# The first image's stages placed four rounds earlier in a hand-made software pipeline

## What is computed

```python
x = x + conv_attention(group_norm(x))   # 1x1 qkv, 5x5 depthwise + grouped 1x1, linear attention, 1x1, batch norm
x = x + conv3x3(group_norm(x), sign(weight))
t = to_tokens(x)                        # 256 tokens x 64
t = t + attention(layer_norm(t))        # 16 heads, three branches: causal, 128 selected tokens, window 32
t = t + moe(layer_norm(t))              # 8 experts, top 2 per token
t = t + linear_attention(layer_norm(t)) # 8 heads of 16
t = t + moe(layer_norm(t))              # 8 experts, routing by image; needs the mean over tokens, and
                                        # the expert loads over all eight images
```

## Time and profile before

| | us |
|---|---|
| median of three runs | 1038.12 |
| lowest and highest | 1030.46, 1038.23 |
| the profiled execution | 1033.71 |
| its span | 1031.8 |
| PE busy | 895.3 (87%) |
| DVE busy | 598.2 (58%) |
| ACT busy | 436.4 (42%) |
| POOL busy | 205.0 (20%) |
| mean granted TensorE clock | 0.97 |

### The profile page before, as it was taken

The page is one execution under the profiler, slowest core; times in us unless marked ns, Lnnn a source line. Parts: engine busy times, 40 slices in busy tenths (PEclk is TensorE's granted clock), DMA queues, the critical chain, the costliest instruction groups (busy, mean ns, idle before and its releaser), DMA issues.

```text
span 1031.8 us, 22157 instructions
## 1 busy us (share of the span) xinstructions
PE 895.3 (87%) x9150; PEld 613.3 (59%) x9150; DVE 598.2 (58%) x1687; ACT 436.4 (42%) x734; POOL 205.0 (20%) x274
## 2 busy tenths in 40 slices
PE   5878789899989899989988999899899989877877
PEld 4766565566656666666656666566565655644553
DVE  6353545663597358745875477637773655462456
ACT  0002235443454245425543464445445535524654
POOL 1011100120123012311241124102411231140122
PEclk9999899999999999999999999999999989997988
DMA  7000000000000000000100000100000000021000
GB/s 190 2 6 1 1 7 21 22 22 26 22 22 23 26 22 22 23 27 6 30 30 26 1 22 27 37 2 22 22 26 23 26 32 23 21 69 30 2 1 22
DMA packets 27140, 25.31 MB, mean 25 GB/s; under 512 B 16480, under 2 KB 22240, under 8 KB 26912
## 3 DMA queue, kind: packets, MB, share of 16 engines
q1 hardware_dynamic: 27040, 23.90, 8.1%
HBM read 19.16 MB, written 4.72 MB: 23 GB/s over the span
## 4 chain that ended last, share of the span: by engine, by line
PE 63%; DVE 18%; ACT 9%; issue 5%; DMA 2%; POOL 2%; SPq 0%; DVEq 0%; POOLq 0%; ACTq 0%
PE ring L904 9%; PE side_a L624 5%; PE pv L943 5%; PE pv L925 4%; ACT pr L1160 4%; PE ring L859 4%; PE heads L847 3%; DVE rden L1639 3%; PE side_a L631 2%; PE heads L884 2%; PE ring L899 2%; PE ring L867 2%; DVE img L1357 2%; PE heads L844 2%; PE side_a L668 2%
## 5 line engine op out<-in xcount | busy, mean ns | idle before, releaser
L1160 ACT ACTIVATE pr<-ring 128x1024 f32<-128x1024 f32 (+1 forms) x128 | 120.9, 944 | 118.5 <-PE ring L908 64.9
L904 PE MATMUL ring<-kq 64*128 64x256 f32 (+2 forms) x1280 | 137.7, 342 | 0.8 <-ACT kq L1205 0.5
L904 PEld LDWEIGHTS ring<-kq 64*128 64x128 f32 x1280 | 93.0, 188 | 44.9 <-issue 35.8
L1197 ACT ACTIVATE kq<-ring 128x896 f32<-128x896 f32 x64 | 58.8, 919 | 92.7 <-PE ring L859 92.7
L1624 DVE TENSOR_REDUCE toks<-heads 128x2 f32<-128x512 f32 x64 | 44.2, 691 | 86.4 <-PE heads L889 85.2
L1649 DVE SCALAR_TENSOR_TENSOR ob<-pv,all_gates,scale 128x256 f32<-128x256 f32 x96 | 46.3, 482 | 77.5 <-issue 33.3
L1639 DVE RECIPROCAL rden<-pv 128x256 f32<-128x256 f32 x32 | 56.1, 1753 | 40.6 <-PE pv L925 40.6
L1629 DVE TENSOR_REDUCE toks<-heads 128x4 f32<-128x512 f32 x64 | 44.2, 690 | 53.4 <-PE heads L884 53.0
L1205 ACT ACTIVATE kq<-ring 128x256 f32<-128x256 f32 x64 | 24.4, 382 | 115.8 <-PE ring L867 115.8
L559 POOL TENSOR_TENSOR toks<-ta,tb 128x128 f32<-128x128 f32 (+1 forms) x96 | 40.3, 439 | 160.2 <-DVE tb L1614 160.2
L859 PE MATMUL ring<-early,toks 128*128 128x128 f32 x448 | 62.2, 279 | 11.2 <-ACT pr L1160 10.5
(11 more groups left out here) (379 smaller groups left out, 1763.5 us busy)
## 6 DMA issues: line engine op xcount, KB each, us to landing
scale<-branch_scale SPq DMA_DIRECT2D x128, 96.0 KB, 2.3
branch_scale<-rden SPq DMA_DIRECT2D x32, 128.0 KB, 1.7
late<-in_late SPq DMA_DIRECT2D x1, 2158.5 KB, 8.3
xin<-in_x SPq DMA_DIRECT2D x16, 64.0 KB, 2.2
pr<-in_prep SPq DMA_DIRECT2D x1, 602.0 KB, 3.8
y<-ob SPq DMA_DIRECT2D x8, 64.0 KB, 1.9
kq<-in_masks SPq DMA_DIRECT2D x1, 480.0 KB, 8.4
toks<-in_final SPq DMA_DIRECT2D x1, 434.0 KB, 4.8
```

The lines of the kernel that those rows point to most:

```text
L904: m = pe.matmul(ring[:, j, at:at + nq], kq[rows, k, key0:key0 + P], kq[rows, k, Q + q_:Q + q_ + nq], start=r % 2 == 0, stop=at > P)
L1160: act.activation(out, in_, ACT.Exp, scale=SCALE).then_inc(S("exp_done"), 1)
L1197: act.activation(kq[:, k, :], flat[:, 0:WIDE], ACT.Copy).then_inc(S("turned"), 1)
```

## The change

The first image's front starts at round -4 instead of 0. Its heads start 16 and its back 48 rounds later than its front, as before, so at 12 and 44 instead of 16 and 48. The other images keep their rounds, and the loop runs from -4.

```diff
-        FRONT_AT = [ROUNDS * n for n in range(B)]
-        HEADS_AT = [ROUNDS * n + ROUNDS for n in range(B)]
-        REST_AT = [ROUNDS * n + 3 * ROUNDS for n in range(B)]
-        TIMES = range(REST_AT[-1] + ROUNDS)
+        LEAD = 4
+        FRONT_AT = [ROUNDS * n - (0 if n else LEAD) for n in range(B)]
+        HEADS_AT = [at + ROUNDS for at in FRONT_AT]
+        REST_AT = [at + 3 * ROUNDS for at in FRONT_AT]
+        TIMES = range(-LEAD, REST_AT[-1] + ROUNDS)
```

## The result

| | before | after |
|---|---|---|
| median, us | 1034.29 (4 runs, 1029.95 to 1038.23) | 1060.97 (4 runs, 1054.40 to 1069.24) |
| ratio after to before, 95% interval | | 1.0263 [1.0167, 1.036] |
| the profiled execution, its span | 1033.71, 1031.8 | 1064.22, 1062.3 |
| PE, DVE, ACT, POOL busy | 895.3, 598.2, 436.4, 205.0 | 915.7, 599.8, 436.1, 204.8 |
| mean granted TensorE clock | 0.970 | 0.947 |

What follows compares the result with a forecast made beforehand. PE was taken as the bound, except in rounds 16 to 31, bound by the second image's serial front chain. Terms +10.3 - 5.8 - 2.4 = +2.1 us gave 1035.8, placed at 1038 towards the runs' median; range 1028 to 1049.

Steps and rivals of the forecast that it cites:

- the worst bound of the sum: Low clock costs again (+4.5), scale loads 3 us more, the back's start 3 us more: +12.6 us.
- the sum of +2.1: Total over rounds 16 to 63: 10.3 - 5.8 - 2.4 = +2.1 us against the profiled execution.
- The path to round 16, parallel from round 64 on, only the three stretches matter: Time up to 70.17 us unchanged, same order from round 64; the whole effect lies between 70 and 335 us.
- Rounds 16 to 31, +10.3: First stretch: 13.2 us of the first image's head work moves in; 63.9 us grows to 74.2.
- At full clock 12.9 + 4.9: Rounds 24 to 27: existing work at full clock plus four fills, and 1.8 of waits, makes 19.6 us.
- The ropes ahead of statistics and image writes: Rounds 16 to 19: DVE's rope products precede the second image's statistics and image writes; its conv starts 4.8 us later.
- Rounds 32 to 47, -5.8: Second stretch: 13.2 us of head work leaves, 3.8 us of denominators and weighings enters; net -5.8 us.
- The new wait for the scale load: Rounds 36 to 39: the second weighing has too little other PE work ahead of it; 2 us of new wait.
- Rounds 48 to 63, -2.4: Third stretch: PE work falls 3.8 us, 1.4 lost as the first image's back precedes the fourth image's mean; -2.4 us.
- The front's chain takes the work for nothing: Rival: idle time in rounds 16 to 31 absorbs the moved work; 1027 to 1032 us; chance 0.12.
- The clock: Rival: clock falls to half again in rounds 24 to 27; +4.5, total +6.6, 1042 us; chance 0.18.
- The collision at round 48: Rival: rounds 48 to 51, a late scale load stalls the fourth image's front; over +10 us; chance 0.12, including several waits.

Runs made afterwards that it cites:

- e1: The change, but the first image's back stays at round 48, so only its front and heads start four rounds earlier; ratio to before 1.0143, mean span 1045.6 us.
- e2: The change, but POOL takes the first image's 5.4 us power two rounds later; ratio to before 1.0195, mean span 1051.4 us.
- f1: The change, but DVE does the second image's statistics and image writes ahead of the ropes in rounds 16 and 17; ratio to before 1.0244, mean span 1056.6 us.
- f2: The change without the filler matmuls of the second image's front; ratio to before 1.0183, mean span 1050.3 us.
- g1: The change with back left at round 48, DVE's statistics and writes ahead of ropes in rounds 16 and 17, no second-image fillers; ratio to before 1.0057.
- f3: The kernel before without the filler matmuls of the second image's front; ratio to before 1.0045, mean span 1036.1 us.

## Why the prediction was wrong

Against the four runs the forecast of 1038 missed by 23, and its range ended 12 us short. The measured change lies beyond the worst bound of the sum too (+12.6). Worked from the profiled executions, the sum of +2.1 stands against +31.4 us at round 64. Two steps failed above all. The low clock of before was taken as gone after the change, 5.3 us that came off the first stretch, and it grew instead. And POOL was not followed to its new place, where its power makes PE wait 5.28 us.

**Step by step.**
- *The path to round 16, parallel from round 64 on, only the three stretches matter.* Right.
- *Rounds 16 to 31, +10.3.* Measured +23.4 in the profiled execution. This is the first step that failed, and its place in the text is "At full clock 12.9 + 4.9": it took the low clock of before (0.89 in this stretch, 5.3 us by the prediction's own figures) as gone after the change. It stayed and grew: 0.82. The sizes at full clock were near, a little low. With 0.38 us for each microsecond at low clock (from e1 and after), the four blocks of after come to 22.8, 11.9, 19.2 and 21.6 us, where the text has 23.4, 12.4, 19.6 and 18.8; the last is off, by 2.8 us. With before's 63.9 brought to full clock in the same way (58.6) the order costs 16.9 us; the text has 15.6, "so 13.2 us of work makes it 15.6 longer". By 0.23, the price in time, it costs 19.5. e1, whose clock of 0.90 is nearly that of before, shows it almost without a correction: 82.64 us and 0.9 from 70.17 to its start, against 63.91, is +19.6. So beside the 5.3 us of clock some 4 us of waits are missing.
- *The ropes ahead of statistics and image writes.* Right in kind, 4.1 us over whole runs.
- *Rounds 32 to 47, -5.8.* +2.3 in after at 0.93. In e1 at 0.98 it is -2.2, some -3.6 at full clock. The new wait for the scale load came (2.15 us, taken as 2), but PE work fell by about 8 instead of 9.4 us.
- *Rounds 48 to 63, -2.4.* +5.7 in after. With the power out of the way and at full clock (e2) it is -1.65, so the term was near for what it counted. This is the second step that failed: it did not count POOL. The prediction followed the back's steps on PE and DVE and named POOL's power only ahead of the writes at round 48. The 5.4 us row was in the trace of before. What was not asked is who stands behind it on POOL in its new place.

Put together at equal clock: +19.6 in the first stretch (from e1), -3.6, -1.65, and +5.3 for the power is +19.6. The whole runs gave +19.0. That the two agree within half a microsecond is partly luck, as the first is made of single executions. The other 8.5 us of the mean are the clock's, by 0.28 us for each of 30.2 us; by the 0.38 seen where PE is the limit it would be 11.5.

**The rivals.** *The front's chain takes the work for nothing* is refuted: PE's idle time in rounds 16 to 31 grew from 15.0 us to 17.1, to 19.2 in e1. The rule of the Trainium skill, "Perfetto Trace Analysis", Optimization Strategy, that interleaving regimes may help, did not pay in this step, which is 2.6% slower. *The clock* was the right mechanism at too small a size: 4.5 us were priced from one block, and all four blocks fell below 0.94. The Trainium skill, "TensorE: Matmul & The Clock Gate", HAM oscillation, says the clock falls where TensorE idles; the runs agree in part: after and its variants with a lead of four rounds and no added fillers have PE idle for 16 to 21 us in rounds 16 to 31 (before 15.0) and average 80 to 106 us at low clock against 71.6. Among them the order is not that of the idle time: e1 with 19.2 us idle has 81.6 us, f1 with 16.5 has 106.2. And the clock at 65.3 fell in a list that had not changed. *The collision at round 48* had the right kind of mechanism (the back four rounds early meets the next image's front) and the wrong engine and round: POOL's power at round 54 to 56, not the scale load.

**What stays open.** Why the time at low clock grew by 30 us: that idle time did it is argued and not shown. How much of f2's 6.1 us is fillers and how much the clock's; which instruction sequence makes the clock fall; and the 4.5 us that are left in g1. Whether the three edits overlap was not followed up.

## What to carry to other kernels

When a stage is moved along a fixed schedule, list for each engine, the little used ones too, what stands behind its longest instruction in the new place: a 5.4 us operation on an engine that is 20% busy cost as much as PE gained in rounds 32 to 63. Don't count a low clock of the kernel before as regained; keep it in the sum at the share that it had, and let it fall further where idle time grows. And compare variants at equal clock before a cause is put on an edit: here the ratio of f1 said that next to nothing had changed, while at equal clock it is 4 us faster.

## What the runs showed of the hardware

- One kernel's time at low clock varies between its runs, and its span with it: 0.28 us of span for each microsecond, 0.18 to 0.39 by stretch.
- POOL's power takes 5.4 us on 128x32 elements and 0.55 us on 128x1; this was the costliest single wait of the change (5.28 us on PE).
- A float32 filler matmul of 128x128 is two passes in the records and takes 0.24 us at full clock (f1: 20 passes in 2.40 us) and 0.47 at the low one (f3, at 64.47: 10 passes in 2.34 us).
- Keeping PE busy raised the clock each time and never paid beyond the fillers that before already has: 52 fillers in g1_all_three cost 6.8 us of span, although in the profiled execution their stretch rose from 0.81 to 0.98.
